# First token loads cut into two 64-partition halves on two DMA queues

## The reference, cut to what matters

```python
x = L0_attn_x                                            # 4 x 512 tokens x 512 features, f32
x = x + 0.5 * ffn(layernorm(x))                          # ffn: silu(x Wg) * (x Wu), times Wd; hidden 2048
x = x + gated_scan_layer(layernorm(x))                   # z = x W, four decayed sums over time, layernorm
x = x + 0.5 * ffn(layernorm(x))                          # the same ffn again
```

## Time and profile before

| | before |
|---|---|
| median of three runs | 1022.33 us |
| the profiled execution's own time | 1022.5 us |
| its span (first to last recorded instruction) | 1020.7 us |
| TensorE busy | 1015.2 us, 99% |
| VectorE, ScalarE, GpSimd busy | 66%, 40%, 16% |
| mean rate of the DMA engines | 213 GB/s |
| first statistics on VectorE begin | 4.51 us |
| first transposes of tokens begin | 8.54 us |

### The profile page before, as it was taken

The page is one execution under the profiler, slowest core; times in us unless marked ns, Lnnn a source line. Parts: engine busy times, 40 slices in busy tenths (PEclk is TensorE's granted clock), DMA queues, the critical chain, the costliest instruction groups (busy, mean ns, idle before and its releaser), DMA issues.

```text
span 1020.7 us, 12555 instructions
## 1 busy us (share of the span) xinstructions
PE 1015.2 (99%) x4512; PEld 841.5 (82%) x4512; DVE 670.9 (66%) x1013; ACT 406.2 (40%) x667; POOL 161.5 (16%) x187
## 2 busy tenths in 40 slices
PE   9999999999999999999999999999999999999998
PEld 8888888888888888888888888888888888888887
DVE  7755665598988687857978877786685333333342
ACT  6644445455423622224732363231282322222311
POOL 3123343125300200210430020021040000000000
PEclk9999999999999999999999999999999999999999
DMA  6588877678767555646856764454677665655255
GB/s 206 226 321 322 300 265 255 227 247 273 242 227 230 182 183 162 202 144 235 271 167 229 235 218 149 147 186 142 229 247 223 211 190 194 204 196 189 87 191 183
DMA packets 61710, 217.89 MB, mean 213 GB/s; under 512 B 6352, under 2 KB 15568, under 8 KB 53968
## 3 DMA queue, kind: packets, MB, share of 16 engines
q1 hardware_dynamic: 61072, 216.03, 62.9%
q10 hardware_dynamic: 576, 1.05, 0.3%
HBM read 170.92 MB, written 46.14 MB: 213 GB/s over the span
## 4 chain that ended last, share of the span: by engine, by line
PE 98%; DMA 1%; DVE 1%; issue 0%; DVEq 0%; SPq 0%
PE ps_a L1534 8%; PE ps_a L1535 8%; PE ps_a L1536 8%; PE ps_b L1534 8%; PE ps_b L1535 8%; PE ps_b L1536 8%; PE ps_c L1534 7%; PE ps_c L1535 7%; PE ps_c L1536 7%; PE ps_d L1534 6%; PE ps_d L1535 6%; PE ps_d L1536 6%; PE aux L1534 3%; PE aux L1535 3%; PE aux L1536 3%; PE ps_d L1696 1%
## 5 line engine op out<-in xcount | busy, mean ns | idle before, releaser
L1031 DVE TENSOR_TENSOR tmp<-tmp,ps_c 128x512 f32<-128x512 f32 x59 | 40.4, 685 | 139.6 <-PE ps_c L1536 139.6
L1534 PE MATMUL ps_a<-xt,gu 128*128 128x512 f32 x304 | 118.3, 389 | 0.0
L1536 PE MATMUL ps_a<-xt,gu 128*128 128x512 f32 x304 | 118.3, 389 | 0.0
L1535 PE MATMUL ps_a<-xt,gu 128*128 128x512 f32 x304 | 118.3, 389 | 0.0
L1535 PE MATMUL ps_b<-xt,gu 128*128 128x512 f32 x286 | 111.3, 389 | 0.0
L1536 PE MATMUL ps_b<-xt,gu 128*128 128x512 f32 x286 | 111.3, 389 | 0.0
L1534 PE MATMUL ps_b<-xt,gu 128*128 128x512 f32 x286 | 111.3, 389 | 0.0
L1536 PE MATMUL ps_d<-dn,hid 128*128 128x512 f32 x256 | 99.6, 389 | 0.0
L1534 PE MATMUL ps_d<-dn,hid 128*128 128x512 f32 x256 | 99.6, 389 | 0.0
L1535 PE MATMUL ps_d<-dn,hid 128*128 128x512 f32 x256 | 99.6, 389 | 0.0
L1536 PE MATMUL ps_c<-xt,gu 128*128 128x512 f32 x236 | 91.8, 389 | 0.0
(11 more groups left out here) (204 smaller groups left out, 2125.4 us busy)
## 6 DMA issues: line engine op xcount, KB each, us to landing
dn<-dn_kept SPq DMA_DIRECT2D x112, 512.0 KB, 3.9
gu<-gu_kept SPq DMA_DIRECT2D x46, 1024.0 KB, 5.0
gu<-gu_kept SPq DMA_DIRECT2D x46, 768.0 KB, 5.5
gu_kept<-gu SPq DMA_DIRECT2D x14, 1024.0 KB, 4.4
gu_kept<-gu SPq DMA_DIRECT2D x14, 768.0 KB, 4.2
dn_kept<-dn SPq DMA_DIRECT2D x16, 512.0 KB, 5.1
h_t<-w_ffn_in SPq DMA_DIRECT2D x18, 256.0 KB, 4.8
x_tok<-w_ffn_in SPq DMA_DIRECT2D x18, 256.0 KB, 5.1
```

Source lines behind the costliest of these rows:

```text
L1031: dve.tensor_tensor(dst, u3s(si), p5_bank(si)[:, :], ALU.add).then_inc(c22_done, 1)
L1534: pe.matmul(dst, a_hi, b_hi, start=start, stop=False, skip_group_check=chained)
L1535: pe.matmul(dst, a_hi, b_lo, start=False, stop=False, skip_group_check=chained)
L1536: return pe.matmul(dst, a_lo, b_hi, start=False, stop=stop, skip_group_check=chained)
```

## The change

Units 0 to 3 are no longer asked for whole. SyncE's queue asks for partitions 0 to 63 of each of them (four DMAs of 128 KB in a row), and ScalarE's queue for partitions 64 to 127 of each (four more). Both halves of a unit add to the same semaphore, so that VectorE's wait for such a unit is for 32. Units 4 and 6 stay whole on SyncE's queue, units 5 and 7 whole on ScalarE's; stage 0 on SyncE's queue comes after four DMAs where it came after two, units 5 and 7 on ScalarE's after four where they came after two.

```diff
+            def load_x_half(r):
+                sp.dma_start(x_tok[0:P // 2, r, :], x_v[0, 0:P // 2, r, :]).then_inc(x_unit[r], 16)
...
-            load_x_unit(0)
-            load_x_unit(2)
+            for r in range(4):
+                load_x_half(r)
             load_stage(0)
             load_x_unit(4)
             load_x_unit(6)
...
-            for r in (1, 3, 5, 7):
-                act.dma_start(x_tok[:, r, :], x_v[r // ST, :, r % ST, :]).then_inc(x_unit[r], 16)
+            for r in range(4):
+                act.dma_start(x_tok[P // 2:P, r, :], x_v[0, P // 2:P, r, :]).then_inc(x_unit[r], 16)
+            for r in (5, 7):
+                act.dma_start(x_tok[:, r, :], x_v[1, :, r % ST, :]).then_inc(x_unit[r], 16)
...
-                        dve.wait_ge(x_unit[r], 16)
+                        dve.wait_ge(x_unit[r], 32 if r < 4 else 16)
```

## The result

The changed kernel is **slower: 1023.92 us**, median of 22 runs, against 1022.19 for the kernel before (also 22), a ratio of 1.0019 with a 95% interval of 1.0013 to 1.0025: small, but clear of the noise. That is 1.7 us more, where 0.5 less was forecast. The runs also scatter more: 1023.37 to 1024.66 with two near 1026 (1026.03 and 1026.06), against 1022.04 to 1022.38 before.

A forecast was written before the change was run, and what follows sets the result against it. TensorE was taken as the bound after 8.54 us, the first normalised tokens before it; the gain was min(0.6 from unit 0, 0.46 from unit 1, 0.63 from TensorE) = 0.46 us, giving 1021.9 us, range 1021.3 to 1022.8.

The forecast's parts named there:

- What bounds the kernel: TensorE is busy from 8.54 us to the last matmul; the change moves only the head, whose gain reaches the end whole.
- Unit 0 earlier: Load of unit 0: lands at 3.9 instead of 4.49 us, moving VectorE's start by 0.6 if taken alone.
- Unit 1 about where it was: Load of unit 1: lands at 4.63, at most 5.05; VectorE begins it at 4.65 instead of 5.11, allowing 0.46 us.
- Units 2 and 3 "not binding": Loads of units 2 and 3: land near 5.1 and 5.7, before VectorE's turns at 5.77 and 6.36.
- The second rival: Units 0 to 3: halves move slower, at worst half of 400 GB/s, head 1.6 us later, 1023.9; chance 10%.
- The issue side: SyncE's queue: two more issues put stage 0 at most 0.86 us later, covered by the queue's backlog; costed at nothing.
- The cap by the dummy matmuls: TensorE before its first transpose: dummy matmuls end at 7.91, so the head can shorten by at most 0.63 us.
- Less than 2.0 us from no change: Whole-kernel verdict: measurement tells about 0.2%, 2.0 us, from no change; same 97%, slower 2%, faster 1%.

The follow-up runs named there:

- by columns: Against the changed kernel, halves of units 0 to 3 cut each token's row, keeping all 128 partitions with 1 KB each: 1021.94 us, ratio 0.9998 to the kernel before.
- the run with paced issues: Against the halves by columns, later halves held back by waits for eight small GpSimd memsets, no DMA added: 1022.46 us.

## Why the prediction was wrong

**What bounds the kernel:** right. The head alone moved, and reached the end nearly whole.

**Unit 0 earlier:** right, 3.84 against 3.9.

**Unit 1 about where it was (4.63):** wrong, 5.15; the stated upper bound was 5.05. **Units 2 and 3 "not binding":** wrong; unit 3 landed at 8.19 against 5.7, VectorE waited 1.10 us for it, and the head was 1.4 late behind it.

The step that failed is one sentence: "Both queues carry a half each at the same time, lower and upper partitions together, so I take the rate of the whole units for the pair". The trace of before couldn't show it for 64 partitions, and I took for fact that two halves issued together pass like one whole unit. What the runs show in its place: cut by partitions unit 3 lands at 8.19, cut by columns at 6.53, with the same number of DMAs and the same bytes. About 0.5 of the loss is the dear issue; of the rest, slow packets are the smaller part and parts of a unit that lag the larger (a spread of 2.4 us between the first and the last of unit 3's increments, against 0.57 before and 1.0 by columns). With two units in one DMA the halves even move in turns, at 229 to 241 GB/s. Why the parts of a partial set lag stays open.

The second rival (1023.9, unit 3 at 8.4, stage 0 at 10.3) came close: 1023.92, unit 3 at 8.19, stage 0's cast at 10.22. In part that is luck. It priced a rate of 200 GB/s, and the changed kernel moved 258 to 290 between 2.7 and 6.3 us; units 0, 1 and 2 landed at 3.8, 5.15 and about 6.4 against its 4.5, 5.8 and 7.1; and halves of every second partition were as slow without its cause. What brought unit 3 to the same place were the late issues and the lag, which it didn't have. Still, the range ended 1.1 us below the result although this price had been worked out: a chance of 10% was too small for a rate that no row showed.

**The issue side, "costed at nothing", upper bound as much as a whole unit:** the bound was wrong (0.58 to 0.86 against 0.43 to 0.47), stage 0 went out 1.6 later instead of 0.86, and it isn't nothing: about 0.5 by the run with paced issues. Holding stage 0 alone cost nothing (1022.00), so it comes through the later halves.

**The cap by the dummy matmuls:** not tested by the change, which never came near it; by columns it was just reached. But their end isn't fixed at 7.91, as the 0.63 assumed: it lay between 7.3 and 8.8 us for the same 18. The matmuls follow each other at 213 ns at first and at 112 ns later, and the change comes where the trace's record of the granted clock (1.00) begins, at 5.91 us in the kernel before, 6.82 by columns, 7.52 in the changed kernel, and between 4.65 and 7.78 over the runs with 18 dummies (ahead of that the trace has no record, and the views print 1.00 as well). No run says what sets that moment.

**Less than 2.0 us from no change:** by the median it is 1.7 us, inside, as given 97%. But the limit itself was too wide: with 22 runs each the interval is 0.06% to either side, and the loss is clear of the noise.

## What to carry to other kernels

If a load on the critical path is cut at all, cut it along the free dimension, so that each piece still has all 128 partitions: that lost nothing here, though its gain (0.26 us) wasn't clear of the noise, while pieces of 64 partitions lost 1.3 us and more in every form tried. DMAs issued together on two queues need not be moved together; before counting on it, look at packets by queue in short stretches, and at how far the first and the last increment of a semaphore lie apart. A mean rate shows neither. And a head that is lengthened can be paid twice, where TensorE's clock falls in it.

## What was unexpected of the hardware

Among the first issues, a DMA of 64 rows took 0.56 to 0.9 us to issue, and one of 128, 96 or 32 rows 0.33 to 0.51 (a whole load right behind a half took 0.56 to 0.84); no run says why. Behind one split unit a single increment of 16 came 1.2 to 2.5 us late, in unit 3 and in the following loads of SyncE's queue, whole ones too. Two loads of 2 KB each, as 256 packets of 16 bytes, among the first transfers (and the Silu table load earlier than else) made those behind them land 1.5 to 3 us later (the second halves by columns at 6.0 instead of 4.34, the fourth at 9.5 instead of 6.5).
